# A four-layer graph network on one core: bf16 one-hot digits, tanh for gelu, other buffers, sweep ends and stage ends

## Time and profile before

| | |
|---|---|
| median of 3 runs | 10061.57 us (10060.24 to 10063.58) |
| profiled execution, its own time | 10059.76 us |
| its span | 10058.0 us |
| busy | PE 1997.3 us (20%), DVE 5828.1 (58%), ACT 3071.7 (31%), POOL 6847.6 (68%) |

### The profile page before, as it was taken

The page is one execution under the profiler, slowest core; times in us unless marked ns, Lnnn a source line. Parts: engine busy times, 40 slices in busy tenths (PEclk is TensorE's granted clock), DMA queues, the critical chain, the costliest instruction groups (busy, mean ns, idle before and its releaser), DMA issues. The chain is left out here.

```text
span 10058.0 us, 59982 instructions
## 1 busy us (share of the span) xinstructions
PE 1997.3 (20%) x16162; PEld 1843.8 (18%) x16162; DVE 5828.1 (58%) x9520; ACT 3071.7 (31%) x3309; POOL 6847.6 (68%) x7186
## 2 busy tenths in 40 slices
PE   4555465651000000002500008000022000110002
PEld 3555465551000000002500007000022000100002
DVE  8777565553545554556588886788874322432225
ACT  6333143331223332232354543355431000110002
POOL 2777777777777777775477763677734777667773
PEclk9999955555555555556855558555555555555556
DMA  3511011111333333334466655566642333223332
GB/s 95 208 29 28 24 44 33 33 31 53 98 99 114 113 109 105 108 110 139 166 212 213 215 183 172 187 217 209 217 124 65 107 103 107 87 90 107 103 107 58
DMA packets 490844, 1161.90 MB, mean 116 GB/s; under 512 B 184121, under 2 KB 279692, under 8 KB 432396
## 3 DMA queue, kind: packets, MB, share of 16 engines
q0 software_dynamic: 255936, 474.70, 18.1%
q1 hardware_dynamic: 204620, 628.82, 16.6%
q10 hardware_dynamic: 29952, 54.54, 2.1%
HBM read 669.61 MB, written 487.92 MB: 115 GB/s over the span
## 5 line engine op out<-in xcount | busy, mean ns | idle before, releaser
L832 POOL DMA_INDIRECT slots<-REC,plc_idx x1664 | 1597.9, 960 | 554.3 <-issue 505.6
L1238 POOL DMA_INDIRECT l_swp_G<-table,KVI x1664 | 1573.3, 945 | 529.1 <-issue 506.3
L940 POOL DMA_INDIRECT l_G<-table,OTHI x1664 | 1581.6, 951 | 513.3 <-issue 506.2
L1490 POOL DMA_INDIRECT l2s_G<-table,OTHI x832 | 785.0, 944 | 428.9 <-issue 253.3
L1490 POOL DMA_INDIRECT l3s_G<-table,OTHI x832 | 786.2, 945 | 301.6 <-issue 253.3
L703 PEld LDWEIGHTS plc_pr<-plc_seen,plc_otf 128*128 128x128 f32 x3328 | 848.4, 325 | 21.3 <-issue 12.1
L703 PE MATMUL plc_pr<-plc_seen,plc_otf 128*128 128x49 f32 x3328 | 849.9, 410 | 11.1 <-DVE plc_seen L618 11.0
L1073 DVE TENSOR_TENSOR l_LB<-l_RE,l_G 128x64 f32<-128x64 f32 x104 | 29.4, 282 | 1024.7 <-DMA l_G<-table,OTHI 1024.5
L1340 DVE SCALAR_TENSOR_TENSOR l_swp_QS<-l_swp_QS,KEEP,l_swp_QX 128x128 f32<-128x128 f32 x1664 | 588.4, 354 | 36.0 <-DMA l_swp_QX<-queries 8.3
L1099 DVE TENSOR_TENSOR_SCAN l_X<-l_AW,l_X 128x2244 f32<-128x2244 f32 x104 | 502.5, 4831 | 3.6
L1399 DVE TENSOR_TENSOR_SCAN l_swp_X<-l_swp_AW,l_swp_X 128x2244 f32<-128x2244 f32 x104 | 501.4, 4821 | 0.1
(11 more groups left out here) (491 smaller groups left out, 9751.1 us busy)
## 6 DMA issues: line engine op xcount, KB each, us to landing
sums<-l_ROW SPq DMA_DIRECT2D x104, 1088.0 KB, 4.3
sums<-l_swp_ROW SPq DMA_DIRECT2D x104, 1088.0 KB
l_swp_QX<-queries SPq DMA_DIRECT2D x104, 1024.0 KB, 7.8
queries<-plc_zrow SPq DMA_DIRECT2D x33, 1664.0 KB
sums<-l3s_ROW SPq DMA_DIRECT2D x52, 1032.0 KB, 4.3
plc_low<-low_rows ACTq DMA_DIRECT2D x208, 256.0 KB, 3.4
sums<-l2s_ROW SPq DMA_DIRECT2D x52, 1024.0 KB, 4.4
table<-t_row SPq DMA_DIRECT2D x98, 512.0 KB
```

Source lines behind the costliest of these rows:

```text
L832: pool.indirect_dma_start(out=slots, out_offset=bass.IndirectOffsetOnAxis(ap=idx[:, c % IB, j:j + 1], axis=0), in_=g.REC[:, c * CH + j, :] ...
L940: pool.indirect_dma_start(out=G[:, c % GR, j, :], out_offset=None, in_=table, in_offset=bass.IndirectOffsetOnAxis(ap=g.OTHI[:, side(c), x: ...
L1238: pool.indirect_dma_start(out=G[:, c % GR, j, :], out_offset=None, in_=table, in_offset=bass.IndirectOffsetOnAxis(ap=index[:, c * CK + j:c ...
L1490: pool.indirect_dma_start(out=G[:, c % GR, j, :], out_offset=None, in_=table, in_offset=bass.IndirectOffsetOnAxis(ap=g.OTHI[:, k, c * CK + ...
```

## The change

- The digits `DIG` are stored in bf16, low and high digits in planes of their own; a second copy of the low digits, `LOW`, stays in f32 for ScalarE's bias and for a transposition.
- One-hot tiles are laid out `[128, CH/4, width, 4]`: four columns lie together innermost. The iota is stored with each value four times (`iota_s` in SBUF for counting; 512 columns of `fixed` in PSUM for placing), so `compare` has an innermost run of four in each operand. TensorE reads a column of such a tile at a step of four (`column`).
- The counting stage has eight buffers (OB) in place of three, and ScalarE makes the low digit of every fourth chunk, not of every third.
- Gelu is `(tanh(u) + 1) x` with the weight halved beforehand; two scalings and both reciprocals are left out.
- Sweep ends: in layer 0 the last but one chunk is added up before the logits of the last. In attention each half of a chunk's gathers has a semaphore of its own, a chunk's carry comes ahead of the next first product, and the last two chunks are closed in the passes of their own chunks.
- Stage ends: the block is made without GpSimd's drain, and one barrier that clears the semaphores takes the place of clearing and a barrier of all engines.
- Semaphores that indirect transfers raise are taken from the top of the free numbers and are never given back (`landing`).

```diff
     def __exit__(self, *a):
         self.ctx.__exit__(*a)
         if a[0] is None:
-            self.nc.clear_and_free_semaphores(self.sems)
-            self.nc.all_engine_barrier()
+            nc = self.nc
+            numbers = [sem.num for sem in self.sems]
+            nc.multi_engine_barrier([nc.gpsimd.engine, nc.sync.engine, nc.scalar.engine, nc.vector.engine, nc.tensor.engine],
+                                    sems_to_clear=range(min(numbers), max(numbers) + 1))
+            for sem in self.sems:
+                nc.release_semaphore(sem)
...
+    def landing(self, name):
+        return self.nc.alloc_semaphore(f"{self.tag}_{name}", num=max(self.nc.free_semaphores))
...
-        return self.ctx.enter_context(self.nc.Block())
+        return self.ctx.enter_context(self.nc.Block(no_gpsimd_drain=True))
...
 def compare(v, out, iota, number):
-    full = [P, out.shape[1], out.shape[2]]
-    return v.tensor_tensor(out, iota.rearrange("p (o w) -> p o w", o=1).to_broadcast(full),
-                           number.to_broadcast(full), ALU.is_equal)
+    full = [P, CH // IN, out.shape[2], IN]
+    return v.tensor_tensor(out, iota.rearrange("p (o w i) -> p o w i", o=1, i=IN).to_broadcast(full),
+                           number.rearrange("p (q o i) -> p q o i", o=1, i=IN).to_broadcast(full), ALU.is_equal)
...
 (loading)
-            v.tensor_copy(down_b[:, :], down[:, 0:1].to_broadcast([P, P]))
+            for to in (cuts, g.iota_s):
+                v.tensor_copy(to[:, 0:IN * P].rearrange("p (w i) -> p w i", i=IN),
+                          g.iota[:, :].rearrange("p (w i) -> p w i", i=1).to_broadcast([P, P, IN]))
...
-                v.tensor_copy(g.DIG[:, k, :, 0], lo[:, :])
-                link(v.tensor_copy(g.DIG[:, k, :, 1], hi[:, :]))
+                v.tensor_copy(g.DIG[:, k, 0, :], lo[:, :])
+                v.tensor_copy(g.LOW[:, k, :], lo[:, :])
+                link(v.tensor_copy(g.DIG[:, k, 1, :], hi[:, :]))
...
 (counting, ScalarE)
-            for c in range(2, NCH, 3):
-                if c >= 3:
-                    act.wait_ge(counted, c - 2)
+            for c in range(3, NCH, 4):
+                if c >= OB:
+                    act.wait_ge(counted, c - OB + 1)
                 for x in range(CH):
-                    o = act.activation(olo[:, 2, x, :], g.iota_b[:, :], ACT.Square, scale=-1.0,
-                                       bias=g.DIG[:, k, c * CH + x, 0:1])
+                    o = act.activation(column(olo[:, c % OB, :, :, :], x), g.iota_b[:, :], ACT.Square, scale=-1.0,
+                                       bias=g.LOW[:, k, c * CH + x:c * CH + x + 1])
...
 (layer 0, VectorE)
-            for c in range(NC2 + 1):
-                if c < NC2:
-                    logits(c)
-                if c >= 1:
+            for c in range(NC2):
+                logits(c)
+                if 1 <= c < NC2 - 1:
                     add_up(c - 1)
+                if c >= NC2 - 2:
+                    add_up(c)
...
 (attention, GpSimd and VectorE)
-                        ...).then_inc(gathered[c % GR], 16)
+                        ...).then_inc(gathered[j // QH][c % GR], 16)
...
             def multiply(c, u):
-                v.wait_ge(gathered[c % GR], 16 * CK * (c // GR + 1))
+                v.wait_ge(gathered[u][c % GR], 16 * QH * (c // GR + 1))
...
-            between = {0: (last_maximum, 0), 1: (maximum, 0), 2: (shift, 0), 3: (fall, 0), 4: (cut, 0),
-                       5: (weigh, -1), 6: (add_up, -1), 7: (carry, -1)}
-            for c in range(-1, NCK + 1):
+            front = {0: last_maximum, 1: maximum, 2: shift, 3: fall, 4: cut}
+            close = {5: weigh, 6: add_up, 7: carry}
+            close_now = {QH + 4: weigh, QH + 5: add_up, QH + 6: carry}
+            for c in range(-1, NCK):
                 for x in range(CK):
                     if c + 1 < NCK:
                         query(c + 1, x)
-                        if x == QH - 1:
-                            multiply(c + 1, 0)
-                    if x in between:
-                        step, back = between[x]
-                        if 0 <= c + back < NCK:
-                            step(c + back)
+                    if c >= 0 and x in front:
+                        front[x](c)
+                    if c >= 1 and x in close:
+                        close[x](c - 1 if c < NCK - 1 else c)
+                    if c == NCK - 2 and x in close_now:
+                        close_now[x](c)
+                    if c + 1 < NCK and x == QH - 1:
+                        multiply(c + 1, 0)
...
 (gelu, VectorE and ScalarE)
                 elif j == 1:
                     v.wait_ge(squared, G + 1)
-                    link(v.scalar_tensor_tensor(out=sq, in0=sq, scalar=1.0 / c0, in1=x, op0=ALU.add, op1=ALU.mult))
-                    v.tensor_scalar(sq, sq, -2.0 * c * c0, 80.0, ALU.mult, ALU.min).then_inc(ready, 1)
-                elif j == 2:
+                    v.scalar_tensor_tensor(out=sq, in0=sq, scalar=1.0 / C0, in1=x, op0=ALU.add, op1=ALU.mult).then_inc(ready, 1)
+                elif j == 3:
                     v.wait_ge(rooted, G + 1)
-                    link(v.tensor_scalar(sq, sq, 1.0, None, ALU.add))
-                    link(v.reciprocal(sq[:, 0:3, :], sq[:, 0:3, :]))
-                elif j == 3:
-                    link(v.reciprocal(sq[:, 3:GT, :], sq[:, 3:GT, :]))
-                elif j == 4:
-                    v.tensor_tensor(x, x, sq, ALU.mult).then_inc(normed, 1)
+                    v.scalar_tensor_tensor(out=x, in0=sq, scalar=1.0, in1=x, op0=ALU.add, op1=ALU.mult).then_inc(normed, 1)
...
-                        act.activation(SQ[:, G % 2, :, :], SQ[:, G % 2, :, :], ACT.Exp).then_inc(rooted, 1)
+                        act.activation(SQ[:, G % 2, :, :], SQ[:, G % 2, :, :], ACT.Tanh, scale=C1 * C0).then_inc(rooted, 1)
```

More of the change, by code:

```diff
@@ L18 @@
 CH = 8
+IN = 4
 GT = 7
@@ L26 @@
 CB = 3
+OB = 8
 assert NCH % IB == 0
@@ L35 @@
 BIG = 1.0e30
+C0 = 0.044715
+C1 = 0.7978845608028654
 RW = 4
@@ L236, in _, with column @@
                 z = min(P, WR - q * P)
-                o = pe.transpose(g.reset[:, q * P:q * P + z], cut_b[0:z, q, :], g.ident_b[0:z, 0:z])
+                o = pe.transpose(g.fixed[:, q * P:q * P + z], cut_b[0:z, q, :], g.ident_b[0:z, 0:z])
             o.then_inc(drawn_p, 1)
 def digit_chunk(g, k, c, half):
-    return g.DIG[:, k, c * CH:(c + 1) * CH, half:half + 1]
+    return g.DIG[:, k, half, c * CH:(c + 1) * CH]
+def column(digits, j):
+    return digits[:, j // IN, :, j % IN]
 def counted_at(c):
@@ L682, in tally_up @@
                 for j in range(CH):
-                    last = pe.matmul(pd[:, j * NB:(j + 1) * NB], olo[:, c % 2, j, :], ohi[:, c % HB, j, :],
-                                     start=True, stop=True)
+                    last = pe.matmul(pd[:, j * NB:(j + 1) * NB], column(olo[:, c % 2, :, :, :], j),
+                                     column(ohi[:, c % HB, :, :, :], j), start=True, stop=True)
                 last.then_inc(tally, 1)
@@ L711, in count_more @@
                 for j in range(CH):
[L712 to L713 removed]
+                    last = pe.matmul(pc[:, 0:NB], column(clo[:, c % CB, :, :, :], j), column(chi[:, c % CB, :, :, :], j),
+                                     start=False, stop=False, skip_group_check=True)
                 last.then_inc(counted, 1)
@@ L858, in layer0_sweeps @@
     with Space(nc, tag) as s:
-        gathered = [s.sem(f"gathered{r}") for r in range(GR)]
+        gathered = [s.landing(f"gathered{r}") for r in range(GR)]
         used, flagged, shifted, powered, summed, carried, rowed, chain = (s.sem(x) for x in (
@@ L1603, in turn_layer @@
     with Space(nc, tag) as s:
-        fetched = [s.sem(f"fetched{q}") for q in range(NG)]
+        fetched = [s.landing(f"fetched{q}") for q in range(NG)]
         masks_ok = [s.sem(f"masks_ok{q}") for q in range(NG)]
```

108 lines of the change are left out of this document (56 added, 52 removed).

## The result

| | median | runs |
|---|---|---|
| before | 10062.6 us | 4 (10060.2 to 10065.6) |
| after | 9964.4 us | 4 (9962.4 to 9966.3) |

The ratio is 0.9902 (95% interval 0.9885 to 0.9919): faster by 98 us. Forecast were 9907 us in a range of 9870 to 9962, so the kernel is 57 us slower than the forecast and 2 us outside the range. The profiled execution took 9966.3 us (span 9964.6), the highest of the four, against 10059.8 of the one before: 93.5 us less.

A forecast was written before the change was run, and what follows sets the result against it. GpSimd's pitch of 1.25 us per gather or scatter was taken to bound the long stages. Terms +1.0 −46 −3.6 −49.8 −4.5 −14 −38 = −154.9 took 10059.8 to 9904.9 us profiled, 9907 forecast, range 9870 to 9962.

The forecast's parts named there:

- Stage ends: Ends of stages: nine exposed GpSimd drains vanish, −49.8 us; bounds all of it or none.
- R1: Rival at stage ends: the drain only moves to the new closing barrier, +49.8 us, 9957; chance 0.12.
- Loading and counting: First stages: two more VectorE copies, +1.0 us; faster 16-bit compares leave ScalarE setting counting's pace, −46 us.
- the bound that left a gain of 19: Counting: if ScalarE's writes at a step of four cost 1.85 ns an element, it has 120 us.
- R3: Rival in counting and placing: compares stay at one element a cycle, +46 + 3.6 us, 9957; chance 0.09.
- Placing: Lead-in of both placing stages: faster compares before the first scatter win 2.2 and 1.4 us, −3.6 in all.
- the compare that the prediction pointed at: First VectorE compare in placing's lead-in, 2.69 us, standing on the way to the first scatter; expected faster.
- Tails: Sweep ends: reordered layer-0 closing −4.5 us; half semaphores and earlier carry −7 in each attention sweep, −14 for two.
- Turn 1 and the closing of layer 2: Tanh gelu: 0 in turn 1, hidden by ScalarE's wait for queries; −38 us in the closing of layer 2.
- R2: Rival in layer 2's closing: closer work lifts TensorE's clock to 2.4 GHz, −25 us, 9882; chance 0.12.
- R4: Rival in placing: faster compares take a memory port GpSimd needs, 0.118 us an issue, +202 us, 10109; chance 0.05.

The follow-up runs named there:

- x1: Changed kernel with its closing barrier replaced by a GpSimd semaphore clear and a semaphore-only barrier, so no drains; 9896.5 us, median of 4.
- x2: Changed kernel with GpSimd's drain put back at the block's end, ahead of the new closing barrier; 9954.2 us, median of 4.
- x8: Changed kernel with semaphore-only stage ends and ScalarE making every fifth chunk's low digit, not every fourth; 9876.9 us, median of 5.
- x5: Changed kernel with one column innermost in place of four, digits still bf16 and broadcast along the innermost dimension; 10007.4 us, one run.
- x7: Changed kernel with runs of four columns kept but the digits stored in f32 as before; 10010.4 us, one run.
- x4: Changed kernel with both half products of an attention sweep waiting for the whole chunk's gathers, new order kept; 9977.5 us, one run.
- x3: Changed kernel with gelu as before (exp, two scalings, two reciprocals) in place of tanh; 10018.2 us, one run.

## Why the prediction was wrong

**Stage ends: the step that failed.** The sum took all 49.8 us "since each engine waits on semaphores of the last transfers before the drain starts". That reason tells that the drain isn't needed, which x1 shows to be right (−67.9 us, with nothing paid in its place). It does not tell that the changed kernel has none. The change removes the drain of the block and ends in a barrier that drains all engines itself; L66's drain of 34 ns on GpSimd stood in the trace of before, and was so short only because L63's had just ended, as x2 shows with 34 ns behind each restored drain. So R1 was the case, and its price was too low: "+49.8" counts the drains that were exposed, but a drain that moves behind the barrier loses its cover in the stages where GpSimd is through early. Twelve stages now show 64.4 us of drain (5.3 + 3.5 + 8.0 + 8.2 + 5.4 + 8.2 + 5.4 + 4.0 + 4.1 + 4.0 + 4.1 + 4.0). In place of −49.8 the term is +14.6 against before: 12.1 are the closing of layer 2, the short layer and the last stage, whose drains had been covered, and 2.6 the attention sweeps' drains, which grew from 4.1 to 5.4 us. x2 gives back about 10 in its median. R1 had a chance of 0.12 and named 9957; with this it would have been 9972, and 9964 was measured.

**Loading and counting** were right: +1.1 for +1.0, −44.8 for −46. The compare came to 0.69 and 0.36 us for "0.63" and "0.29", at no cost, as ScalarE sets the pace as forecast (x8); by the narrow and the wide one together an element costs 0.52 ns (329 ns for 632 elements) for 1.04 before. ScalarE's strided squares add 0.2 us a chunk, far from the bound that left a gain of 19. R3 fell, and x5 and x7 show how near it was: with either of the two conditions missing, the compares are at 1207 and 549 ns and counting is 40.8 us longer.

**Placing** was right in its sum: the first scatter comes 2.5 us earlier in the first stage and 1.1 in the second, 3.6 for 3.6. But the compare that the prediction pointed at, of 2.69 us, didn't get shorter; it ends with GpSimd's clearing of a buffer before and after, and the gain comes from the compares of later chunks. The Trainium skill has two sentences on it ("VectorE: DVE Perf Modes"). The tier table's one element a cycle for a `tensor_tensor` with any PSUM operand is refuted for 16 bits by the 673 ns above (1205 ns in the same stage before); "Why PSUM operands drop a tier", which gives two to 16-bit operands and one to f32, fits both this and the 1205 ns.

**Tails** were right in mechanism: layer 0's is 4.8 us shorter for 4.5, as the trace has it; no run takes that step out alone. An attention sweep's rows come 7.4 us earlier for 7, and with the 1.6 of the last scatter, which I didn't have, less the drain's 1.3 more its stage is 7.9 shorter. x4 takes back 6.5 of it, and 6.5 was expected.

**Turn 1 and the closing of layer 2.** In turn 1 nothing was forecast and 2.8 us came, of which no part is shown to be tanh. In the closing −38 was forecast, −39.8 came without the drain, and −38.9 by x3. R2 was wrong: the granted clock went from 0.52 to 0.54, so the level stayed at 1.2 GHz for nearly all of the stage.

**Layer 0's gathers** are a term that I didn't have. From its first to its last gather the stage takes 2227.0 us, 5.6 more than before, with no edit in that part. All of it is in the durations of the issues: over their median of 944 ns the 1664 issues have 10.8 us together before and 16.4 after, and the idle time between them is 640.7 us in both. It is a matter of when an issue meets a long instruction of VectorE. In the timeline of the kernel after:

```profile
3836.36 1.09 DVE L1161 TENSOR_TENSOR l_SQ<-l_tab_rec,l_rec 128x896 f32<-128x896 f32 x1
3836.41 1.85 POOL L960 DMA_INDIRECT l_G<-table,OTHI  x1 [0.31 <-issue]
3837.48 1.09 DVE L1166 TENSOR_TENSOR HH<-HH,l_SQ 128x896 f32<-128x896 f32 x1
...
3838.57 0.94 POOL L960 DMA_INDIRECT l_G<-table,OTHI  x1 [0.30 <-issue]
```

and at such a place in the kernel before:

```profile
3950.02 1.09 DVE L1141 TENSOR_TENSOR l_SQ<-l_tab_rec,l_rec 128x896 f32<-128x896 f32 x1
3950.88 1.05 POOL L940 DMA_INDIRECT l_G<-table,OTHI  x1 [0.30 <-issue]
```

The issue takes 1.85 us in one and 1.05 in the other, for 0.94 elsewhere, and in both it ends 0.82 us after VectorE's product does (3838.26 − 3837.45, 3951.93 − 3951.11). It waits for the product's end, and how long depends on where in the product it falls. The stage has seven of these products (L1161, L1141 before): six hold up an issue after, by 4.4 us together, and five before, by 0.7. The scans of 832 elements hold up eight issues in each kernel, to 1.4 to 2.5 us apiece. This is the kind of hold that R4 feared, from instructions that the change doesn't touch. "SBUF: two separate sides" of the Trainium skill's page "SBUF — State Buffer" says it this way, whichever of the two starts first taking the shared ports for its whole instruction. For a product of two inputs in SBUF the trace agrees as far as the issue waits; the other way round it doesn't, since products that start 0.2 to 0.8 us into an issue take 1.09 us like the rest. The compares didn't bring it: placing issues are 961 ns for 960. Over the profiled runs with gathers of 0.945 to 0.946 us, from this kernel's 2227.0 to x8's 2221.9, this part varies by 5 us with the same code in it, so the 5.6 us are in part chance. What sets the moment at which the two meet was not tried.

**The sum redone** with what was measured: +1.1 − 44.8 − 3.6 + 14.6 − 4.8 + 5.6 − 18.4 (attention tails, without the drains' growth) − 2.8 − 39.8 = −92.9 against −93.5 of the profiled executions; the rest is turn 0 (−0.9), the plain sweeps (−0.3) and the last stage without its drain (+0.6). Against the forecast of −154.9, stage ends are 64.4 us worse, layer 0's gathers 5.6 worse, the attention tails 4.4 better, and all other terms together 4 better.

## What to carry to other kernels

Before a cost is struck out because an edit removes its instruction, look for another instruction that would inherit the wait: a drain of 34 ns behind a drain of 5 us is cheap only in that company, and a rival that says "it only moves" should be priced with the covers that it loses, not at zero. A compare on VectorE took half the time per element once each operand was of 16 bits and had pairs that lie together, the broadcast one too; lay tiles out for it, and divide the work between the engines anew afterwards.

## What the runs showed of the hardware

- GpSimd's drain behind indirect transfers takes 3.5 to 8.2 us, and 17.6 to 22.6 when it starts right behind 49 fetches; in this kernel nothing after it needs it (x1: 67.9 us less and no later issue longer for it). Right behind another drain it takes 34 ns (x2).
- TensorE's granted clock in the first placing is 0.50 (the 1.2 GHz level) in the kernel after and in every run with fast compares, and 1.00 (2.4 GHz) in the kernel before, x5 and x7, where the compares are slow, at nearly equal TensorE time. Windows of that stage, after and x5:

```profile
127.00:1201.00 1074.00, 606.42 (x4998) 591.14 (x4998) 598.86 (x1160) 338.89 (x312) 799.82 (x833) 0.50 0.29 85
```

```profile
168.00:1244.00 1076.00, 597.50 (x4998) 581.52 (x4998) 750.78 (x1159) 338.70 (x312) 799.26 (x833) 1.00 0.28 85
```

  The 2.4 GHz level was kept from counting on in x5 and lost within it in the kernel after (0.62 over the counting stage, 1.00 before). In the latter it fell at 48 us, after TensorE had been busy 10.2 of 18 us; in x5 it was busy 9.0 of the same 18 us and the level stayed. It cost 9 us of TensorE's busy time and none of the stage's (1074.6 us after, 1077.3 in x5), which GpSimd paces. Why the denser counting loses it stays open.
- GpSimd's gathers took 0.948 us and not 0.945 throughout two profiled executions (x2, x3), which is some 14 us of this kernel's time.
- An indirect issue of GpSimd that starts within an f32 product of VectorE (1.09 us, both inputs in SBUF) ends about 0.8 us after the product; it took up to 1.86 us for 0.94.
